# Two residual blocks on one core: another order of offset convolution, sampling and norms

## What is computed

```
out = relu(group_norm(conv1x1(x, w1), 32 groups))            # 64 channels
om  = conv3x3(out, w_off) + b_off                            # 27 channels: 9 dx, 9 dy, 9 masks
sampled[k] = bilinear(out, grid_y+ky+dy[k], grid_x+kx+dx[k]) * sigmoid(mask[k])   # 9 taps
out = relu(group_norm(sum over k of w2[k] . sampled[k], 32 groups))
x   = relu(group_norm(conv1x1(out, w3), 32 groups) + x)      # 256 channels
```

## Time and profile before

| | us |
|---|---|
| median of 3 runs | 95.29 (95.27 to 95.33) |
| the profiled execution, its own time | 95.34 |
| its span, first to last instruction | 93.6 |
| PE busy | 76.0 |
| DVE busy | 67.3 |
| ACT busy | 51.5 |
| POOL busy | 5.0 |

### The profile page before, as it was taken

How to read it: one execution, slowest core, us unless ns; L and a number is a source line. 1 busy time by engine, 2 the same in 40 slices (tenths; PEclk the granted TensorE clock), 3 DMA queues, 4 the chain that set the end, 5 groups by cost and what they waited for, 6 DMA issues and landing times.

```text
span 93.6 us, 2197 instructions
## 1 busy us (share of the span) xinstructions
PE 76.0 (81%) x894; PEld 52.0 (56%) x894; DVE 67.3 (72%) x185; ACT 51.5 (55%) x92; POOL 5.0 (5%) x10
## 2 busy tenths in 40 slices
PE   4999999995898989999999797969269689595500
PEld 1325765574797779899778664434124276381100
DVE  1125359999999999994089535985898876849960
ACT  4102372989949998748990026404654244734760
POOL 7500110000000000000002200000000000000000
PEclk9999999999999999999999999999999999999955
DMA  2999700000000000000000000000000000000066
GB/s 15 320 331 294 310 3 0 0 7 0 0 7 0 0 7 0 7 7 0 0 7 0 0 0 7 0 0 0 0 0 0 0 0 0 4 7 0 0 232 217
DMA packets 3274, 4.17 MB, mean 45 GB/s; under 512 B 256, under 2 KB 2688, under 8 KB 3264
## 3 DMA queue, kind: packets, MB, share of 16 engines
q1 hardware_dynamic: 2992, 3.76, 12.7%
q10 hardware_dynamic: 272, 0.26, 0.8%
HBM read 2.98 MB, written 1.05 MB: 43 GB/s over the span
## 4 chain that ended last, share of the span: by engine, by line
DVE 37%; PE 36%; ACT 16%; issue 6%; DVEq 0%; ACTq 0%
PE acc L462 8%; PE slot L341 6%; ACT g_cols L690 6%; DVE g_rows L871 5%; PE acc L588 5%; PE slot L449 3%; PE acc L352 3%; DVE g_cols L962 3%; DVE g_cols L1008 3%; DVE stats L926 3%; ACT g_cols L774 3%; PE slot L377 2%; DVE hats L840 2%; ACT pad L743 2%; ACT hats L657 2%
## 5 line engine op out<-in xcount | busy, mean ns | idle before, releaser
L871 DVE TENSOR_TENSOR g_rows<-hats 128x2304 f32<-128x2304 f32 (+1 forms) x12 | 20.5, 1752 | 0.1
L690 ACT ACTIVATE g_cols<-slot 128x768 f32<-128x768 f32 x24 | 18.0, 825 | 2.6 <-PE slot L449 2.6
L462 PE MATMUL acc<-g_cols,v_sb 128*64 128x128 f32 x288 | 18.1, 276 | 0.4 <-ACT g_cols L690 0.4
L462 PEld LDWEIGHTS acc<-g_cols,v_sb 128*64 128x64 f32 x288 | 15.5, 137 | 1.5 <-ACT g_cols L690 0.8
L449 PE MATMUL slot<-consts_sb,g_rows 64*128 64x64 f32 x288 | 12.0, 226 | 1.9 <-DVE g_rows L871 1.2
L341 PE MATMUL slot<-zeros 128*128 128x512 bf16 x41 | 12.0, 430 | 1.2 <-DVE zeros L793 1.2
L449 PEld LDWEIGHTS slot<-consts_sb,g_rows 64*128 64x128 f32 x288 | 10.4, 140 | 3.7 <-issue 1.9
L341 PEld LDWEIGHTS slot<-zeros 128*128 128x128 bf16 x41 | 4.1, 108 | 6.1 <-issue 2.7
L341 PE MATMUL acc<-zeros 128*128 128x512 bf16 x25 | 6.2, 379 | 0.0
L743 ACT ACTIVATE pad<-g_cols 64x256 bf16<-64x256 int8 x8 | 3.3, 418 | 4.8 <-DVE g_cols L1008 4.7
L377 PE MATMUL slot<-feat,woff_sb 128*64 128x256 f32 x36 | 4.7, 385 | 0.0
(11 more groups left out here) (127 smaller groups left out, 122.0 us busy)
## 6 DMA issues: line engine op xcount, KB each, us to landing
out<-g_cols SPq DMA_DIRECT2D x4, 256.0 KB, 2.3
x_sb<-x SPq DMA_DIRECT2D x3, 256.0 KB, 4.0
wq_sb<-wq SPq DMA_DIRECT2D x1, 484.5 KB, 6.4
woff_sb<-woff SPq DMA_DIRECT2D x1, 288.0 KB, 5.5
w_sb<-w SPq DMA_DIRECT2D x1, 288.0 KB, 5.6
x_sb<-x ACTq DMA_DIRECT2D x1, 256.0 KB, 3.3
w_sb<-w SPq DMA_DIRECT2D x1, 256.0 KB, 6.5
consts_sb<-consts SPq DMA_DIRECT2D x1, 232.0 KB, 5.5
```

Source lines behind the costliest of these rows:

```text
L462: mm = nc.tensor.matmul(acc[b2][rows(h), at:at + P], v_sb[:, B2 * h + b2, q, k, :], g_cols[t][h][:, NQ * k + q, :], start=(k == 0 and q == ...
L690: nc.scalar.activation(dst.rearrange("p k (r n) -> p k r n", r=HALVES), src.rearrange("p r (k n) -> p k r n", k=per), ACT.Copy).then_inc(g ...
L871: tt(g_rows[i % 3][:, taps], hats[:, t, h, 1, taps].unsqueeze(3).to_broadcast(shape), hats[:, t, h, 0, taps].unsqueeze(2).to_broadcast(sha ...
```

## The change

Order and banks change; what is computed does not.
- The offset convolution of the first pair goes ahead of the second pair's pair sums. The second pair's variance, root, scale and normalisation come later: the scale after `differences(0)` on DVE, the normalisation on ACT after the first mask. The second offset convolution comes after v0 to v3.
- Every product is made in thirds, both halves alternating: (0,0), (1,0), (0,1), ... for each t, and turned in that order.
- v0 to v3 get banks of their own. v4 to v7 all go to `acc[1]`, late in the sampling, after turn 5 and tap 6, each waiting for the copy of the one before. The last taps of each pair are made and copied apart, the second pair's in `acc[1]` too.
- `om_turn(1)` comes between turns 1 and 2, into `acc[1]`.
- On ACT `distance(2)` and `distance(3)` follow copies 8 and 11, not 5 and 8; the signs, the table load and `root(3, 0)` move too.
- On DVE `moments(0)` comes ahead of the last six thirds, `pair_var` and `pair_scale` among them; the batch norm's six instructions and all passes over wq follow the last third.
- After conv3(0) PE samples on to the end without interruption; conv3(1) writes to other banks, so that its first part need not wait for the norms of the first pair. The norms of conv3(0) and of the second pair's sampled output run in alternation, and the residual sums are split around `eight_moments(1)`.
- From the third quantised convolution on, one matmul spreads the bias ahead of the convolution, and one reduction over 256 columns takes the place of two over 128.

The core of the diff (unchanged renamings and helper signatures left out):

```diff
-WHOLE = UNITS - HALVES
-THIRDS = tuple((i, j) for i in range(WHOLE) for j in range(TURNS)) + tuple(
-    (WHOLE + h, j) for j in range(TURNS) for h in range(HALVES))
+ROOT_AT, NORMALISE_AT = 20, 21
+THIRDS = tuple((HALVES * t + h, j) for t in range(T) for j in range(TURNS) for h in range(HALVES))
...
+        v_banks = (small[0], acc[0][:], slot[0][:, 0:BANK], small[1]) + (acc[1][:],) * B
...
+            om(0)
+            pair_sums(2, 1)
+            pe.wait_ge(consts_in, 16)
+            om_turn(0)
+            pe.wait_ge(w2_in, 16)
+            make_v(0)
+            make_v(1)
+            make_v(2)
+            pe.wait_ge(omt_ready, 1)
+            make_last_v(0)
+            pe.wait_ge(gn_ready, 4)
+            make_v(3)
+            om(1)
...
-            turns(0, 5)
-            sample(0, 0, 4)
+            turns(0, 1)
+            om_turn(1)
+            turn(2)
+            sample(0, 0, 2)
+            turns(3, 5)
+            pe.wait_ge(omt_ready, 2)
+            make_last_v(1)
+            sample(0, 3, 6)
+            for i in range(B, 2 * B):
+                pe.wait_ge(v_ready, i + 2)
+                make_v(i)
             turns(6, 8)
-            sample(0, 5, 6)
+            sample(0, 7, 8)
+            sample(1, 0, 0)
             turns(9, 11)
-            sample(0, 7, 8)
-            sample(1, 0, 3)
+            sample(1, 1, 6)
             turns(12, 14)
-            sample(1, 4, 6)
+            sample(1, 7, 8).then_inc(sampled, 1)
+            pe.wait_ge(v_ready, 2 * B + 2)
+            sample(2, 0, 0)
             turns(15, 17)
-            sample(1, 7, 8).then_inc(sampled, 1)
-            sample(2, 0, 3)
+            sample(2, 1, 6)
             turns(18, 20)
             pair_sums(3, 0)
-            sample(2, 4, 6)
+            sample(2, 7, 8)
+            sample(3, 0, 0)
             turns(21, 23)
-            sample(2, 7, 8)
-            sample(3, 0, 1)
+            sample(3, 1, 2)
...
             conv3(0)
-            sample(3, 2, 5)
+            sample(3, 3, 8).then_inc(sampled, 1)
             eight_means(0)
-            sample(3, 6, 7)
             eight_vars(0)
-            sample(3, 8, 8).then_inc(sampled, 1)
+            pair_sums(5, 1)
             pe.wait_ge(std_ready, 4)
-            idle(IDLE[3], acc[0][:])
-            pair_sums(5, 1)
             idle(IDLE[4], acc[0][:])
             conv3(1)
...
             for n in range(len(THIRDS)):
                 copy_g(n)
+                if n == 1:
+                    copy_omt(1)
+                if n == 4:
+                    copy_last_v(1)
                 if n == 5:
+                    for i in range(B, 2 * B):
+                        copy_v(i)
+                if n == 8:
                     distance(2)
-                if n == 10:
+                if n == 11:
+                    distance(3)
+                if n == 14:
                     a.wait_ge(wq_in, 16)
...
+            pair_var(2, 1)
+            dve.wait_ge(omt_done, 1)
+            nc.vector.tensor_copy(omt_sb[:, 0].rearrange("p q h o -> p (q h o)"), omt_of(0)
+                                  ).then_inc(omt_ready, 1)
+            before_next(differences(0))
+            pair_scale(2, 1, V_GN1S, V_GN1B)
+            make_hats(0)
+            apply_mask(0)
+            make_g(0, 0)
+            make_g(1, 0)
+            add_grid(1)
...
+            apply_mask(3)
+            dve.wait_ge(sampled, 1)
+            moments(0)
+            make_g(6, 0)
+            make_g(7, 0)
+            make_g(6, 1)
+            make_g(7, 1)
+            pair_var(3, 0)
+            make_g(6, 2)
+            pair_scale(3, 0, V_GN2S, V_GN2B)
+            make_g(7, 2)
             dve.wait_ge(bn_std_ready, 1)
             settle(nc.vector.reciprocal(bn_std[:], bn_std[:]))
...
             eight_moments(0)
-            eight_scale(0)
-            norm3(0)
             dve.wait_ge(sampled, 2)
             moments(1)
+            eight_scale(0)
             pair_var(5, 1)
             pair_scale(5, 1, V_GN2S, V_GN2B)
-            residual(0)
+            norm3(0)
+            add_residual(0, ((3, 0), (0, 1)))
             eight_moments(1)
-            first_half_max(1, LEAST_MAX)
+            add_residual(0, ((1, 2), (2, 3)))
+            largest(0)
             eight_scale(1)
             norm3(1)
-            last = residual(1)
+            first_half_max(1, LEAST_MAX)
+            add_residual(1, ((3, 0), (0, 1), (1, 2), (2, 3)))
+            last = largest(1)
             settle(last)
             make_scale(1)
...
-                first_half_max(n, LEAST_MAX)
-                make_scale(n)
+                make_scale_of_both(n)
```

More of the change, by code:

```diff
@@ L277, in inner, with omt_of, last_v_of, conv3_out @@
             return tile[:, b2, 1:1 + H, 1:1 + W]
+        def omt_of(b2):
+            return (slot[1] if b2 == 0 else acc[1])[:, 0:NQ * CB]
+        v_banks = (small[0], acc[0][:], slot[0][:, 0:BANK], small[1]) + (acc[1][:],) * B
+        def last_v_of(b2, h):
+            return slot[1][:, BANK * h:BANK * h + NQ * CB] if b2 == 0 else acc[1][:, NQ * CB * h:NQ * CB * h + NQ * CB]
         def image(t):
             return t.rearrange("p (y x) -> p y x", y=H)
-        def conv3_out(c, h):
-            return slot[h][:, BANK * c:BANK * c + N]
+        def conv3_out(c, h, b2):
+            if b2 == 1 and c == 0:
+                return acc[h][:, 0:N]
+            bank = c * (1 - b2)
+            return slot[h][:, BANK * bank:BANK * bank + N]
+        def vars_of(b2):
+            return acc[0][:, 0:4] if b2 == 0 else slot[1][:, BANK:BANK + 4]
         def sums_of(n, b2):
             return acc[0][:, N:N + 8] if n == 3 else small[b2][:, 0:8]
+        spread = [small[0][:, P + P * b2:2 * P + P * b2] for b2 in range(B2)]
         def rows(h):
@@ L392, in _, with om @@
             pe.wait_ge(woff_in, 16)
-            for b2 in range(B2):
+            def om(b2):
                 pe.wait_ge(feat_ready, b2 + 1)
@@ L424, in _, with make_last_v @@
[L424 to L429, removed]
-                make_v(i)
-                mm = make_last_v(i)
-            mm.then_inc(v_done, 1)
+            def make_last_v(b2):
+                pe.wait_ge(flat_ready, b2 + 1)
+                for h in range(HALVES):
+                    if b2 == 1 and h == 1:
+                        pe.wait_ge(v_done, B + 3)
+                    for q in range(NQ):
+                        at = N * b2 + P * q
+                        mm = nc.tensor.matmul(last_v_of(b2, h)[:, CB * q:CB * q + CB], feat_flat[rows(h), at:at + P],
+                                              w2_sb[rows(h), BANK:TAPS * CB], start=True, stop=True)
+                    mm.then_inc(v_done, 1)
@@ L439, in turn @@
                 if n < TURNS:
-                    pe.wait_ge(v_ready, (5, 6, 2 * T + 1)[n])
+                    pe.wait_ge(v_ready, (4, 5, 5)[n])
                 else:
@@ L590, in window_conv @@
                     mm.then_inc(qconv_done, 1)
-                for b2 in range(B2):
-                    spread_bias(n + 1, b2)
                 spread_max(n + 1, 0)
@@ L631, in _ @@
             normalise(1, 0, inner(feat, 0), image(acc[0][:, 0:N]), feat_ready)
-            root(2, 1)
-            normalise(2, 1, inner(feat, 1), image(acc[1][:, 0:N]), feat_ready)
             def copy_om_rest(b2):
@@ L876, in _ @@
             add_grid(0)
+            pair_var(2, 1)
[9 more added lines that the diff above has]
+            add_grid(1)
+            make_g(0, 1)
+            make_g(1, 1)
+            make_g(0, 2)
+            make_g(1, 2)
+            settle(differences(1))
+            make_hats(1)
+            apply_mask(1)
+            make_g(2, 0)
+            make_g(3, 0)
+            make_g(2, 1)
+            differences(2).then_inc(diff_ready, 1)
+            make_g(3, 1)
+            make_g(2, 2)
+            make_g(3, 2)
+            differences(3).then_inc(diff_ready, 1)
+            apply_mask(2)
+            for j in range(TURNS):
+                make_g(4, j)
+                make_g(5, j)
+            apply_mask(3)
[9 more added lines that the diff above has]
+            make_g(7, 2)
             dve.wait_ge(bn_std_ready, 1)
```

178 lines of the change are left out of this document (74 added, 104 removed).

## The result

| | before | after |
|---|---|---|
| median, us | 95.28 | 101.1 (99.70 to 103.05, 4 runs) |
| ratio, 95% interval | | 1.056 (1.046 to 1.067) |
| profiled execution, its time and span | 95.34, 93.6 | 103.05, 101.3 |
| TensorE's mean granted clock in it | 0.974 | 0.918 |

The change costs 5.8 us: slower, as forecast, but 3.2 more than the forecast of 97.9 and outside the range. Ratios and their intervals leave out executions more than 1.5% above the fastest of their kernel (here the 103.05, in run 3 the 101.16 and 102.06, in run 9 the 144.41), medians don't.

A forecast was written before the change was run, and what follows sets the result against it. It took PE as nearly full in the sampling stretch, with short dependent steps after it. Against 95.34 us, +5.9 to conv3's moments, -2.8 to the second spread and -0.5 for scales gave +2.6, so 97.9, range 95.8 to 99.0.

The forecast's parts named there:

- Start: Up to the first product: an earlier offset convolution and moved batch norm bring it to 16.3 us instead of 17.03.
- The round in one bank: v4 to v7 in acc[1]: product, copy and hop take 1.80 us a round, so turn 6 starts at 33.3, not 27.23.
- (a): Rival on the v rounds: only throughput counts, 1.34 us a round, time 96.5 us; chance 0.14.
- (b): Rival on the v rounds: the bank costs only the products, 0.86 us a round, time 95.1 us; chance 0.12.
- DVE's path to the moments: DVE from distance(2) through thirds, batch norm and wq passes: moments of conv3 at 56.6 instead of 50.66, 5.9 us later.
- From there to the second spread: From conv3's moments to the spread of the second maximum: 13.8 us instead of 16.6, a gain of 2.8.
- The scales: Both later quantised convolutions: one reduction over both halves saves 0.25 us each, bounds 0.1 to 0.4, together 0.5.
- The changes of kind on PE: Some five more changes between turns and samples: up to 0.8 us, 0.3 counted; if all cost, about 98.5.
- the sum: Whole kernel against the profiled execution: +5.9 - 2.8 - 0.5 = +2.6, giving 97.9 us.
- rival (c): TensorE's clock falls to 1.2 GHz: each v takes 0.86 us longer, 3.4 in four, time 101.3; chance 0.07.
- theory A: From the experiments: the order costs what the sum says, 97.9 us; thinly used PE in one-bank rounds lowers the clock.

The follow-up runs named there:

- run 3: The changed kernel once more, unaltered, to see where its clock falls: 100.52 us, ratio 1.049.
- run 9: The kernel of run 8 with 15 idle products for 7 ahead of the second spread: 93.12 us, ratio 0.979.
- run 1: The changed kernel with three idle matmuls after each of v4, v5, v6, in the gaps of the one-bank rounds: 99.79 us, ratio 1.050.
- run 6: Run 1 with the batch norm's instructions and four passes over wq moved into DVE's wait ahead of the mask for t=2: 97.41 us, ratio 1.024.
- run 7: Run 4 with batch norm and one wq pass ahead of the mask, two passes in the wait for the pair sums: 93.89 us, ratio 0.989.
- run 5: The kernel before with v4 to v7 all in one bank, each waiting for the copy before: 99.76 us, ratio 1.045.
- run 2: Run 1 with 15 idle products for 7 ahead of the second spread: 99.66 us, ratio 1.046.
- run 4: The changed kernel with v4 to v7 in four banks instead of one: 95.79 us, ratio 1.008.
- run 8: The kernel before with only the change's part from conv3(0) on, the new scales included: 93.17 us, ratio 0.980.
- run 10: The kernel before with only the new scales: one bias spread ahead of the convolution and one reduction: 94.50 us, ratio 0.995.
- run 11: Run 8 with the remaining passes over wq in DVE's wait for the root of the second group norm: 93.27 us, ratio 0.981.
- run 12: Run 11 with the second pair's samples in two parts and the means' product between them: 93.21 us, ratio 0.977.

## Why the prediction was right in its direction and wrong in its size

- **Start**: right. First product at 16.41 (16.3), DVE waits for the second pair's offsets until 19.03 (19.2), v4 at 26.90 (26.9).
- **The round in one bank**: right at the upper clock, 1.81 for 1.80, in the changed kernel and in run 1. Rivals (a) and (b) fall with it. In run 1 the copy of turn 6 starts at 33.91 (34.0).
- **DVE's path to the moments**: right without a fall, 56.63 for 56.6 in run 1. Its 7.55 us from the second pair's variance (51.45) to the moments (59.00) are the forecast's 7.6. That conv3 doesn't bound was right (run 1), but only narrowly: with the passes away the moments wait for conv3 (runs 6 and 7), and behind it the means wait for the samples, so that only 1.0 of the 2.0 us saved on DVE arrives.
- **From there to the second spread**: 14.19 (14.20 in run 3) for 13.8, so a gain of 2.4 and not 2.8. The term that was 0.4 too small is the second pair's last sums: from their first product to the norm it takes 2.69 us (67.82 to 70.51) for the 2.27 of the earlier trace rows, since on ACT a pass over the first pair's output (0.63 us from 68.37) stands ahead of the squares. The fall in run 1 cost the stretch 1.2 more.
- **The scales**: from the end of the second raw product to the reciprocal 1.11 us (86.14 to 87.25) instead of 1.29 (78.08 to 79.37): 0.18 each, not 0.25, inside the bounds of 0.1 to 0.4.
- **The changes of kind on PE**: the 0.3 in the sum was enough. Run 1 meets the forecast's 56.6 to 0.03, so the 98.5 that the rule of the Trainium skill (TensorEngine Tiling (Array Packing), Key Properties) gave isn't needed, though the order alone comes near it by other terms; at v4 the weight load stands 0.17 us once more, as in the earlier trace rows.
- **The failed step is rival (c)**, which got 0.07 and lay outside the range; the sum has nothing for a fall of the clock. I set it aside on one row, the 1.78 us of idle PE at 67.22 with the clock up. That row is no evidence about rounds that repeat: here PE worked 1.1 and idled 0.7 us, and the clock fell to 1.2 GHz ahead of the third product (30.1, changed kernel), during the third (22.9, run 5) or during the fourth (32.95, run 3), in all three profiles with the rounds unfilled (changed kernel, runs 3 and 5) and in none of the three with them filled (runs 1, 2, 6). The rule of the Trainium skill (TensorE: Matmul & The Clock Gate, What's actually happening), that idleness brings the throttle back, stood in the prediction beside it; its direction holds at this place. Its price was off too: not 0.86 in each of four products, 3.4, but 2.3 in the changed kernel's profile and 1.2 in run 3, since two or three products were made before the fall, while turns behind them were slowed (33 transposes took 2.88 us, in run 1 1.70). That its 101.3 is so near the median of 101.1 is luck: a price too high for this fall, none for the second, and a sum at least 0.5 short.
- **A second fall was in no step.** From the second spread to the second quotient it takes 8.52 us (73.19 to 81.71), before it took 6.44 (67.22 to 73.66), in the other profile of this kernel (run 3) 6.43, and in all nine profiles without a fall there 6.43 or 6.44: 2.1 us. With 2.4 for the moments (59.00 for 56.6, nearly all the first fall), 0.4 for the stretch ahead of the spread, 0.14 for the scales and the 2.6 of the sum this makes 7.6; the profiled execution is 7.7 longer than the one before. The median, 101.1, lies 2 us lower.

So theory A holds in the main: the order costs 3.1 to 3.3 us (run 6) and not 2.6, for the 0.4 and 0.14 above, and the rest, about 2.5 us in the median, is the clock. Still open: why the second fall comes in one execution and not in another. It also comes in the profiles of runs 4, 7 and 8, there at a cost of 0.4 to 0.7 us; in all four it starts 0.6 to 1.3 us after the second spread. It comes in none of runs 1, 2, 3, 5, 6, 10, 11 and 12, of which the last two are run 8 with two small moves. The gap of 2 us ahead of the spread stands in most of these too, so it doesn't suffice; whether it is needed isn't shown (runs 2, 9), and no run tried other gaps.

The change holds two good parts, the end (2.0 us by run 8, the scales among them) and the earlier start, and two bad ones, the one bank (5.3 by run 4, the clock included) and wq at one place late on DVE (1.0 at the second spread by runs 6 and 7, 1.9 between the medians of runs 4 and 7). The earlier start and the later offsets of the second pair have no run of their own.

## What to carry to other kernels

Where products take turns with their copies in one bank, count the latency of product, copy and hop per round, and then ask what TensorE does in the rest of each round: price the half clock for the rounds and for all that stands behind them, and let it into the range. A single long gap that the clock survived says nothing about many short ones. Count two profiles from the same event before comparing them: v4 is issued at 26.19 in one profile and at 27.36 in another, though the instructions ahead of it are the same. When a change has several parts, run its last independent stage alone: here that was a gain of 2% inside a loss of 6%.

## What the runs showed of the hardware

- The clock can fall with no gap longer than 0.7 us in the rounds before it (changed kernel, 28.0 to 30.1), while the kernel before keeps it through a gap of 1.78 us.
- Idle products are no free remedy: eight of them take 1.90 us at the upper level and 3.32 to 3.47 at the lower one, and they stand ahead of real work (runs 1, 2). Filling one stretch went with a fall in another, 30 us later, in two of three profiles (runs 1 and 2, not 6).
- The fall doesn't come at a fixed place: in the same kernel at 30.1 us in one execution and at 32.95 in another. The eight executions of this kernel spread over 3.6 us (99.42 to 103.05), where most runs here stay within 1. But a fall can also be steady: the four executions of run 5 lie within 0.05 us, all at a mean granted clock of 0.946 to 0.950.
- TensorE starts each execution slowly, though the granted clock is given as 1.00 there: seven idle products take 3.17 us from 1.19 in the profile of the kernel before, later 1.67. Where it gets faster differs by execution: the first convolution's eight records take from 1.26 (run 7) to 1.98 us (the kernel before), and all behind them moves with it. In the execution of 144.41 us (run 9) it never did, and the granted clock is given as 1.00 throughout.
